# First key projection of a delta-rule stage made in the program of the stage ahead of it, and a new order of pieces in every phase of that stage

## The reference, cut to what matters

```python
def short_conv(x, w):                       # 4 taps in time, then silu
    ...
    return jax.nn.silu(y)
def l2norm(x):
    return x * jax.lax.rsqrt(jnp.sum(x * x, axis=-1, keepdims=True) + EPS_L2)
def step(S, inp):                           # one head (12 of them), one token
    qt, kt, vt, gt, bt = inp
    S = S * jnp.exp(gt)
    delta = (vt - kt @ S) * bt
    S = S + kt[:, None] * delta[None, :]
    return (S, qt @ S)
```

## Time and profile before

| what | value |
|---|---|
| median of three runs | 1339.88 us (1336.66 to 1342.13) |
| the profiled execution, its own time | 1341.76 us |
| its span | 1340.0 us, 25269 instructions |
| PE / DVE / ACT / POOL busy | 92% / 61% / 41% / 40% of the span |
| the delta stage, from its first matmul to the next stage's | 452.79 to 824.65 us, 371.9 us |

### The profile page before, as it was taken

The page is one execution under the profiler, slowest core; times in us unless marked ns, Lnnn a source line. Parts: engine busy times, 40 slices in busy tenths (PEclk is TensorE's granted clock), DMA queues, the critical chain, the costliest instruction groups (busy, mean ns, idle before and its releaser), DMA issues. The chain is left out here.

```text
span 1340.0 us, 25269 instructions
## 1 busy us (share of the span) xinstructions
PE 1229.2 (92%) x9232; PEld 784.1 (59%) x9232; DVE 815.8 (61%) x1828; ACT 555.6 (41%) x1333; POOL 531.1 (40%) x628
## 2 busy tenths in 40 slices
PE   7999999949686898999999887999999989999998
PEld 4969687737454644666666654455555554444487
DVE  5474746466443668777877536777777783734253
ACT  4545546333123397777777440444444331000010
POOL 3543526650572288568668512422222211600010
PEclk9999999968798799999999987999999999999999
DMA  4010109363895401313222201000002007642000
GB/s 137 25 34 5 39 22 335 111 236 139 245 283 194 133 20 21 49 30 64 37 38 32 37 6 46 22 22 30 32 23 75 1 3 195 196 134 71 23 9 24
DMA packets 144265, 106.60 MB, mean 80 GB/s; under 512 B 87968, under 2 KB 130184, under 8 KB 143008
## 3 DMA queue, kind: packets, MB, share of 16 engines
q1 hardware_dynamic: 137632, 88.50, 23.4%
q0 software_dynamic: 4496, 13.33, 3.7%
q10 hardware_dynamic: 2032, 3.35, 0.8%
HBM read 84.16 MB, written 22.35 MB: 79 GB/s over the span
## 5 line engine op out<-in xcount | busy, mean ns | idle before, releaser
L3250 PE MATMUL la_banks<-la_xe,la_f_w 128*128 128x512 f32 x348 | 153.1, 598 | 3.5 <-DVE la_xe L3628 3.5
L3791 POOL TENSOR_TENSOR la_area<-la_area 128x512 f32<-128x512 f32 x48 | 60.3, 1279 | 173.3 <-DVE la_area L3471 153.0
L2494 DVE SCALAR_TENSOR_TENSOR dh_front<-dh_pj,df_conv,dh_front 128x510 f32<-128x510 f32 x144 | 106.9, 745 | 22.9 <-ACT dh_front L2124 19.2
L3250 PEld LDWEIGHTS la_banks<-la_xe,la_f_w 128*128 128x128 f32 x348 | 66.0, 192 | 84.7 <-issue 84.6
L353 POOL TENSOR_TENSOR wa_qkT<-lf_area 128x512 f32<-128x512 f32 x40 | 50.8, 1271 | 96.7 <-DVE lf_area L325 96.7
L3628 DVE TENSOR_TENSOR la_xe<-xT,la_area 128x1024 f32<-128x1024 f32 x29 | 52.6, 1828 | 57.0 <-PE la_banks L3250 49.8
L3368 ACT ACTIVATE la_area<-la_banks,la_nmax 128x256 f32<-128x256 f32 x128 | 59.0, 475 | 58.6 <-DVE la_nmax L3480 58.6
L357 POOL TENSOR_TENSOR mw_gu<-mw_gu,const 128x384 f32<-128x384 f32 x64 | 63.7, 1000 | 29.9 <-ACT mw_gu L388 29.9
L3811 POOL TENSOR_TENSOR la_o_rstd<-la_o_var,la_minus_half 128x1 f32<-128x1 f32 x8 | 6.4, 804 | 166.0 <-DVE la_o_var L3690 166.0
L3376 ACT COPY la_area<-la_banks 128x512 f32<-128x512 f32 x64 | 37.5, 590 | 56.2 <-PE la_banks L3099 55.9
L280 PE MATMUL wa_po<-wa_wo,mw_rows 128*128 128x256 f32 x256 | 56.6, 379 | 0.0
(11 more groups left out here) (645 smaller groups left out, 3053.7 us busy)
## 6 DMA issues: line engine op xcount, KB each, us to landing
mw_gu<-in_L_ffn_gate_up SPq DMA_DIRECT2D x16, 768.0 KB, 14.0
placed<-mw_rows SPq DMA_DIRECT2D x8, 768.0 KB, 10.3
mw_d<-in_L_ffn_down SPq DMA_DIRECT2D x16, 384.0 KB, 15.8
mw_rows<-placed SPq DMA_DIRECT2D x8, 768.0 KB, 6.4
la_area<-w_table POOLq DMA_DIRECT2D x6, 1024.0 KB, 12.0
pairs<-me_picked SPq DMA_DIRECT2D x7, 704.0 KB, 3.7
la_f_w<-in_L_ffn_q_proj SPq DMA_DIRECT2D x32, 128.0 KB, 2.3
la_f_w<-in_L_ffn_k_proj SPq DMA_DIRECT2D x32, 128.0 KB, 2.4
```

Source lines behind the costliest of these rows:

```text
L2494: dve.scalar_tensor_tensor(dst, src[:, :, 0:SEQ - j], conv[:, a, m, D_CONV - 1 - j:D_CONV - j], dst, ALU.mult, ALU.add).then_inc(tapped, 1)
L3250: mm = pe.matmul(acc[c][m], f_w[n % SLOTS][:, m, k, :], xe[(n - U) % RING][:, k, :], start=first and k == 0, stop=last and k == KC - 1)
L3791: pool.tensor_tensor(qrot[:, c, n, :], prod[:, c, 2 * n, :], prod[:, c, 2 * n + 1, :], ALU.add).then_inc(rotated, 1)
```

## The change

One unit of work moves to another program, and most calls of the delta stage are put in another order. The number of matmuls stays.

**The early unit.** In the expert stage PE makes the first unit of head 0's key projection ahead of the last `turn_x`, from weights that are there and from the half of `xT` that is already copied; ACT keeps it in a tile that lives across the stages. ACT now makes both copies of the first half of `xT`, and DVE's copy of one of them goes away.

```diff
+                pe.wait_ge(first.w_loaded, 32)
+                pe.wait_ge(copied, 2)
+                pe.wait_ge(complete, 6)
+                for k in range(KC):
+                    mm = pe.matmul(tp[:, 0, :], first.w[:, 0, k, :], env.xT[:, k, 0:512], start=(k == 0), stop=(k == KC - 1))
+                mm.then_inc(first.early_done, 1)
                 turn_x(1)
...
-                for th in range(2):
-                    act.wait_ge(turned, 2 * th + 2)
-                    act.copy(env.xT[:, 1, 512 * th:512 * th + 512], (hp, op)[th][:, 1, :]).then_inc(copied, 1)
+                for kc in range(KC):
+                    act.wait_ge(turned, kc + 1)
+                    act.copy(env.xT[:, kc, 0:512], hp[:, kc, :]).then_inc(copied, 1)
+                act.wait_ge(first.early_done, 1)
+                act.copy(lf.area[:, 1536:2048], tp[:, 0, :]).then_inc(first.early_kept, 1)
+                act.wait_ge(turned, 4)
+                act.copy(env.xT[:, 1, 512:1024], op[:, 1, :]).then_inc(copied, 1)
...
                 moments(1)
-                dve.wait_ge(turned, 1)
-                dve.tensor_copy(env.xT[:, 0, 0:512], hp[:, 0, :]).then_inc(copied, 1)
                 scale(1)
...
+        unit = lambda u: pj[:, u % 2, :] if u else lf.area[:, 1536:2048]
...
                 def project(a, n):
                     u, (m, s) = 4 * a + n, divmod(n, 2)
+                    if u == 0:
+                        return
```

**Phase -1 gets an order of its own.** PE starts with unit 1 of head 0 and makes the gates behind it:

```diff
-                    if i < 3:
+                    if i < 0:
+                        if a is not None:
+                            project(a, 1)
                         if i == -1:
                             betas_and_gates()
+                        for n in news[0:1]:
+                            project_v(n)
+                        if a is not None:
+                            project(a, 2)
...
```

**The tail** has a new order on each engine. The diff of PE's at two places, and of DVE's end:

```diff
+                k_products(LAST, 0)
+                solution(7, 1)
+                level6_x(8)
+                turn_solution(7, 1)
+                k_products(LAST, 1)
                 gate(2)
-                level5_y(8)
-                solution(7, 1)
-                k_products(LAST, 0)
-                level6_x(8)
-                k_products(LAST, 1)
-                turn_solution(7, 1)
-                level6_y(8)
                 within(7, 1)
                 k_products(LAST, 2)
                 k_products(LAST, 3)
+                level6_y(8)
...
                 carried(10)
-                level6_y(11)
                 turn_carried(10)
                 out_pair(1)
                 solution(10, 1)
+                level6_y(11)
...
                 second_out(11)
-                sum_out(11)
                 gate_last(0)
                 gate_last(1)
+                sum_out(11)
```

More of the change, by code:

```diff
@@ L1871, in _ @@
                             k_products(b, 1)
+                        for n in olds[1:2]:
+                            turn_v(n)
+                        if b is not None:
                             k_products(b, 2)
@@ L1886, in _ @@
                         if b is not None:
+                            turn(b, 0)
                             turn(b, 1)
@@ L1906, in _ @@
                             project(a, 2)
+                        if b is not None:
+                            k_products(b, 0)
                         for h in chain_heads(i):
@@ L2590, in _ @@
                     a, b, f = heads(i + 1), heads(i), heads(i - LAG_NORM)
-                    if i < 3:
-                        if b is not None:
-                            sums(b, 0)
+                    if i < 0:
+                        if a is not None:
+                            taps(a, 0)
+                            taps(a, 1)
                         if i == -1:
@@ L2596, in _ @@
                             log_decay()
+                        if a is not None:
+                            taps(a, 2)
+                            taps(a, 3)
+                    elif i < 3:
                         if b is not None:
+                            sums(b, 0)
                             sums(b, 1)
@@ L2879, in _ @@
                             norms(b)
+                        if f is not None:
+                            invert_out(f)
+                        if a is not None:
+                            mask_e(a, 0)
+                        if f is not None and f < 8:
+                            norm_out(f)
                         if a is not None:
```

323 lines of the change are left out of this document (172 added, 151 removed).

## The result

The changed kernel took 1350.31 us in the median of four runs (1343.74 to 1354.66), the kernel before 1338.27 (1334.13 to 1342.13, four runs): a ratio of 1.0077 with a 95% interval of 1.0047 to 1.0107. Timed twice more beside the kernel before it gave 1.0036 (1.0011 to 1.0060) and 1.0077 (1.0049 to 1.0106), so the change costs 5 to 10 us. Executions of one kernel differ by 10 to 20 us here, in both kernels, and the profiled one of the change is the fastest of its four (1343.74). The ratios leave out executions over 1.5% above the fastest of their kernel: one of the kernel before (1352.82), one of e2_early_only (1355.01), one of e14_hand_fill (1353.62) and two of e15_before_fill (1352.48 and 1352.76).

What follows compares the result with a forecast made beforehand. The prediction took PE to bound phases 3 to 10, with time without PE mainly in phases -1, 2 and the tail. Terms -1.1 - 0.1 - 0.6 + 1.5 - 1.25 = -1.5 gave a median of 1338.4 us, range 1329 to 1345.

Steps and rivals of the forecast that it cites:

- -1.1: Early unit at the hand-over: it fills PE's wait and the last turn stays at 2.4 GHz, 1.1 us gained.
- -0.1: Phase -1, clock low again: first half's exp ends at +26.2 us from the stage's start instead of +26.3.
- -0.6: Phases 0 to 2: nothing in 0 and 1; in phase 2 `project(4, 0)` ahead of the turn gains 0.6 us.
- +1.5: Phases 3 to 10: the solve ends 1.04 us later, so PE waits longer for `dh_U`, 1.5 us lost.
- -1.25: Tail: two `level6_y` calls moved gain 0.9 and 1.0 us, DVE's longer wait for POOL's root costs 0.65.
- 1.09 for 2.29: Hand-over: the last turn takes 1.09 us at full clock instead of 2.29, -1.2, of which -1.1 is handed on.
- the rival in which the clock holds: Phase -1 at 2.4 GHz from its start: log decay at +12.3, exp about +21, 5.3 us more gained, 1333.1; chance 0.20.
- the main sum: Phase -1 in the small sum (chance 0.55): clock low, log decay ends at +16.4 us, first half's exp at +26.2.
- That order stays, so the wait stays: Phase 2: POOL still makes the second `scale_e` after its solve, so PE's 2.98 us wait remains.
- With loads 1.04 later, PE waits 0, 0.45 and 1.05 longer: Phases 4, 6 and 8: PE's added waits for the `dh_U` loads, in sum +1.5 us.
- The record's slower rival: Phases 4, 6, 8, 10: `dh_U` has nothing to spare, each costs 1.04 + 0.5 us, +6.2 for +1.5, 1343.1; chance 0.13.
- Its first part: Tail: `level6_y(8)`, 1.14 us, goes behind the last `k_products`, so DVE's solve comes about 0.9 us earlier.

Runs made afterwards that it cites:

- e2_early_only: The kernel before with the early unit and the new order of phase -1 alone; 0.9975 of before (0.9943 to 1.0006).
- e14_hand_fill: The change with the old orders in phases 3 to 10 and the tail, plus two idle matmuls at the hand-over; 0.9961 of before, median 1337.90 us.
- e15_before_fill: The kernel before with one idle matmul added in the tail ahead of `level4_x(11)`; 0.9983 of before (0.9964 to 1.0002).

## Why the prediction was wrong, step by step

The record had -1.1, -0.1, -0.6, +1.5 and -1.25. Over the profiled executions phases -1 to 2 are shorter by 2.0 (twelve with the new orders and no idle matmul there, mean 86.5; five with the old, 88.5), phases 3 to 10 longer by 5.0 (seven, 194.1; eight, 189.1), and the tail by about 2 (99.6 over eight; 97.7 over six, some of them behind new phases). That is +5 for -1.5. The early parts came out near their sum of -1.8, though not by the steps told; phases 3 to 10 and the tail account for the rest. The tails overlap (95.6 to 102.4, and 93.1 to 101.9), so for the tail the timed kernels above weigh more.

**The early unit** lay in the gap as told: 1.88 us, and 1.34 of idle time left for 1.2. But the turn could not take 1.09. Timeline of the change:

```profile
441.60 1.88 PE L1037 MATMUL me_tp<-xT,df_w 128*128 128x512 f32 x4
...
444.36 1.38 DVE L1279 TENSOR_SCALAR x<-x,me_mv,me_rstd 128x256 f32<-128x256 f32 x4 [1.12 <-POOL me_rstd L1340]
...
444.83 2.15 PE L1023 MATMUL me_op<-const,x 128*128 128x128 f32 x8 [1.34 <-DVE x L1279]
...
449.19 3.75 PE L1700 MATMUL dh_pj<-xT,df_w 128*128 128x512 f32 x4 [2.21 <-PEq L3891]
...
452.74 3.75 PE L1598 MATMUL dh_bd<-df_wab,xT 128*128 128x24 f32 x32
...
456.32 3.61 PE L1613 MATMUL dh_lv<-xT,dh_wv 128*128 128x512 f32 x4
...
461.99 0.33 DVE L2469 SCALAR_TENSOR_TENSOR dh_par<-dh_soft,dh_a_exp 128x96 f32<-128x96 f32 x1
...
470.90 0.63 PE L1719 MATMUL dh_tp<-const,dh_back 128*128 128x128 f32 x4 [1.54 <-ACT dh_E L2162]
```

and the same turn where the change was timed again:

```profile
446.84 1.74 PE L1023 MATMUL me_op<-const,x 128*128 128x128 f32 x8 [1.35 <-DVE x L1279]
```

The turn took 2.15 us for 2.29: the clock was at 1.00 up to 446.0 and fell within the turn. Where it did not fall, as in the second row and in nine of the thirteen profiled kernels with the early unit and no idle matmul at the hand-over, the turn took 1.73 to 1.75. Its first four instructions start 0.32 us apart at either clock, the pace at which DVE's `scale` hands over what they read (four in 1.38 us). The 1.09 of the earlier trace rows is that of a turn that waited for nothing: its instructions start 0.11 us apart, one pair 0.16. So the step that failed is "1.09 for 2.29": a clock that holds is worth 0.55 at most. From the start of the last sum to the stage's first matmul the hand-over takes 7.81 us here for 7.95, and 7.4 where the turn runs at full clock: 0.1 to 0.6 was won and not 1.1. One old hand-over (POOL's order alone) had its turn at full clock too, without the early unit.

**Phase -1** was told as 28 us with a low clock, or 5.3 less with a full one. It came out between, in two forms: 7 to 8 us at half clock in nine executions (23.4 to 24.0 us) and 15 in four (27.3 to 27.5). The four are as told, but for some 0.6 us. In the nine, the group of lines above among them, the first projection ran slow, the clock then rose with the gates (3.75 us for 6.99), and was low again under the values' projection (3.61 for four records). The log decay ended 13.1 us into the stage and PE stood for the exp of the decays to 21.7, near the rival in which the clock holds (12.3 and 21) and not the main sum (16.4 and 26.2), though the rival's condition, a full clock from the start, was not met.

The two added table loads cost what the row said: each load in phase -1 takes 1.28 us and the next activation starts within 0.1 us of its end. The drain that the Trainium skill (ScalarE: Activation LUTs, "What ACT_TABLE_LOAD costs") puts beside a load does not show there. The early unit's 1.88 us did not hold the clock: in the thirteen executions it fell between 3.4 us ahead of the stage's start and 0.3 behind it, and with two idle matmuls more, 1.02 and 0.60 us, the first projection ran at full clock in both profiles. The Trainium skill's rule beside that rival (TensorE: Matmul & The Clock Gate, "What's actually happening": recent activity releases the slow clock) is not contradicted by that.

The gain is half taken back in phase 0, 20.8 for 18.4 in every one of them, which the record did not have: ACT's `tap0` of unit 3 stands behind the sigmoid and the exp, so DVE's taps of it run up to phase 0's start, and PE waits 0.65 us for them and 1.22 for the next ones; before, it waited for neither.

**Phase 2** became 1.8 shorter for 0.6. "That order stays, so the wait stays" did not hold: the wait of 2.98 us is 0.42 in the profiled execution of the change, where the clock was low for 6.8 us of the phase, and 1.7 to 1.9 where it was low for 3.4. The phase took 21.6 to 21.8 us in either case, so here the slow clock only filled the wait.

**Phases 3 to 10** are a term that was mis-sized: +5.0 for +1.5. The mechanism was there: the solve later, `dh_U` late. But the step "With loads 1.04 later, PE waits 0, 0.45 and 1.05 longer" took the solve's start from the moved call alone. PE waited 0.60, 3.43, 2.00 and 0.85 us for the loads of phases 4, 6, 8 and 10. The load of the solve's input was late as well (2.09 us in phase 6), and PE came earlier. The record's slower rival, 4.7 us more than the sum, had this place, and its condition (two more of the four loads late) came true in phases 4 and 10. PE's time without work in these phases (their length less its busy time) is 7.1 us in the mean of the seven, 4.5 in the eight with the old order; time at half clock is 4.9 and 3.4, so the falls in phases 7 and 9 are the smaller part.

**The tail** is the other step that failed, and here the sign was wrong: -1.25 told, +3.0 in the timed kernels with the tail alone (give or take 3.9), about +2 in the profiles. The sum counted each moved call by the time that it no longer takes. Its first part came true and was not handed on. The first step of DVE's last solve, before, and in the change with the last norm (`dh_ms`; that of before is in the earlier trace rows, at 802.76):

```profile
753.51 0.18 DVE L2580 TENSOR_TENSOR dh_tmp<-dh_Ab,dh_Tm 128x15 f32<-128x15 f32 x1 [1.69 <-DMA dh_Ab<-delta_a]
```

```profile
753.01 0.17 DVE L2622 TENSOR_TENSOR dh_tmp<-dh_Ab,dh_Tm 128x15 f32<-128x15 f32 x1 [0.28 <-DMA dh_Ab<-delta_a]
...
804.79 0.41 DVE L2473 TENSOR_REDUCE dh_ms<-dh_own 128x8 f32<-128x256 f32 x1
```

From the tail's start (728.92 and 730.75) the solve begins at 24.6 before and 22.3 in the change, the norm at 73.8 and 74.0: 2.3 us won and lost again in between, up to 1.2 of them because the norm now stands behind two instructions of the gate (counted as 0.65). Nor did PE stand less: its time without work in the tail is 17.2 us in the mean of the eight executions with the new order and nothing added, 16.7 in the six with the old one. What grew is the time at half clock, 35.8 us for 27.1, and that was in no term. The clock fell 38 to 41 us in, in all eight, where `turn_pair(0)` had stood ahead of `level4_x(11)` and its wait for a transfer; moved away, it left a stretch with 0.8 us of work in 2. The idle matmul in that place is worth 5.7 us side by side.

Three things stay open: why the clock falls at one place of the tail and not at another, since the call put back only moved the fall; why a fall lasts 7 us in one execution and 20 in another; and what makes up the 1.6 us of the 5.0 in phases 3 to 10 that PE's longer waits (2.6) and the clock (at most 0.8) leave.

## What to carry to other kernels

When calls move on the engine that bounds a kernel, look at what each one leaves behind: a wait that was covered becomes a thin place, and here one with 1.19 us of wait went with 7 to 20 us at half clock. Ask also whether the time that a moved call saves reaches the end: here the last solve came 2.3 us earlier and the last norm no earlier. Putting one call back may only move the fall; a matmul that nobody reads was cheaper than the gap here. Before a duration is taken from another place of the trace (1.09 us for the turn), see whether the inputs come at the same pace. And where executions differ by more than the effect, take several profiles and sum by stretch, and compare the granted clock of all timed executions, since the profile at hand may be the luckiest.

## What the runs showed of the hardware that was not expected

One added matmul of 1.02 us lowered the time by 5.7 us beside the same kernel without it, and the time at half clock by 16.7. A fall of the clock lasted between 7 and 20 us in the same place of the same kernel; in the long one PE was busy for 1.6 to 2.0 of every 2 us. And the clock fell, rose and fell again within 11 us around the start of phase -1 (446.0, 452.8 and 456.2), though PE was busy without a break from 449.19 to 459.60: slow for the first projection, full for the gates, slow for the values.
